# Cross-attention and feed-forward block: output weights loaded in pieces and split in the last batch, two output tiles projected inside the attention block

## The reference, cut to what matters

```python
q = layernorm(x) @ Wq;  k = ctx @ Wk;  v = ctx @ Wv      # per batch: 112x1024, 375x256, 375x256
out = softmax(q k^T / sqrt(32)) v                        # 4 query heads share one k, v head
x = x + out @ Wo                                         # Wo 1024x1024
x = x + w2( silu(w1 h) * (w3 h) ),  h = layernorm(x)     # width 3584, weights with block scales
```

## Time and profile before

| | us |
|---|---|
| median of three timed runs | 2510.64 |
| the three runs | 2515.27, 2510.57, 2510.64 |
| the profiled execution, whole | 2515.51 |
| its span | 2513.7 |
| PE busy in the span | 2423.2 (96%) |
| DVE, ACT, POOL busy | 1697.5, 979.4, 558.2 |

### The profile page before, as it was taken

How to read it: one execution, slowest core, us unless ns; L and a number is a source line. 1 busy time by engine, 2 the same in 40 slices (tenths; PEclk the granted TensorE clock), 3 DMA queues, 4 the chain that set the end, 5 groups by cost and what they waited for, 6 DMA issues and landing times.

```text
span 2513.7 us, 35414 instructions
## 1 busy us (share of the span) xinstructions
PE 2423.2 (96%) x12682; PEld 2068.6 (82%) x12682; DVE 1697.5 (68%) x2639; ACT 979.4 (39%) x1673; POOL 558.2 (22%) x305
## 2 busy tenths in 40 slices
PE   7998999999999799799999998999999989999999
PEld 7997878878876388699999987999888978888887
DVE  6425777777776445788888887888878874445442
ACT  3212445445454422444544445334443342323221
POOL 1000354454454400011111110332233320000000
PEclk9998999999998799899999999999999999999999
DMA  7534555455545345475565643766577687565652
GB/s 226 173 96 137 144 136 145 134 141 143 133 113 136 85 148 168 126 218 163 175 185 157 179 151 113 207 168 173 189 211 203 169 280 228 171 186 151 186 164 84
DMA packets 369147, 408.04 MB, mean 162 GB/s; under 512 B 125825, under 2 KB 324097, under 8 KB 359153
## 3 DMA queue, kind: packets, MB, share of 16 engines
q1 hardware_dynamic: 369008, 406.22, 56.6%
HBM read 252.99 MB, written 152.70 MB: 161 GB/s over the span
## 4 chain that ended last, share of the span: by engine, by line
PE 47%; DVE 4%; DMA 2%; issue 1%; SPq 0%; ACT 0%; DVEq 0%
PE bank L84 16%; PE bank L86 16%; PE bank L85 16%; DMA stash<-weight_scratch 2%; DVE g_WL L90 1%; DVE g_XL L90 1%; DVE g_su L1731 1%; DVE stash L1225 1%; DVE stash L1226 1%; DVE xT L1723 0%; SPq L1544 0%; DVE stash L1228 0%; ACT stash L1649 0%; DVE stash L1736 0%; ACT g_WH L1198 0%
## 5 line engine op out<-in xcount | busy, mean ns | idle before, releaser
L84 PE MATMUL bank<-g_XH,g_WH 128*128 128x448 f32 (+1 forms) x2254 | 847.1, 376 | 34.4 <-DVE g_su L1731 17.6
L85 PE MATMUL bank<-g_XL,g_WH 128*128 128x448 f32 (+1 forms) x2254 | 844.5, 375 | 0.0
L86 PE MATMUL bank<-g_XH,g_WL 128*128 128x448 f32 (+1 forms) x2254 | 844.4, 375 | 0.0
L84 PEld LDWEIGHTS bank<-g_XH,g_WH 128*128 128x128 f32 x2254 | 424.6, 188 | 98.4 <-DVE g_WL L90 22.4
L86 PEld LDWEIGHTS bank<-g_XH,g_WL 128*128 128x128 f32 x2254 | 424.6, 188 | 54.3
L85 PEld LDWEIGHTS bank<-g_XL,g_WH 128*128 128x128 f32 x2254 | 424.7, 188 | 54.0
L1198 ACT ACTIVATE g_WH<-stash 128x512 fp32r<-128x512 f32 x392 | 241.2, 627 | 420.9 <-PE bank L86 249.5
L90 DVE TENSOR_TENSOR g_WL<-stash,g_WH 128x512 fp32r<-128x512 f32 (+1 forms) x417 | 335.8, 809 | 77.2 <-ACT g_WH L1198 48.9
L696 DVE TENSOR_REDUCE a_nm<-bank 112x1 f32<-112x375 f32 x512 | 265.2, 532 | 116.8 <-PE bank L831 113.2
L800 ACT ACTIVATE a_pr<-bank 125x448 f32<-125x448 f32 x384 | 204.2, 545 | 205.8 <-PE bank L907 151.9
L649 POOL TENSOR_TENSOR a_prsum<-a_pr 125x1792 f32<-125x1792 f32 x32 | 129.4, 4043 | 362.2 <-ACT a_pr L800 362.2
(11 more groups left out here) (132 smaller groups left out, 3589.3 us busy)
## 6 DMA issues: line engine op xcount, KB each, us to landing
stash<-in_L_ffn_w SPq DMA_DIRECT2D x168, 256.0 KB, 5.2
weight_scratch<-stash SPq DMA_DIRECT2D x28, 1024.0 KB, 7.7
stash<-weight_scratch SPq DMA_DIRECT2D x28, 1024.0 KB, 7.4
h_scratch<-g_Sh SPq DMA_DIRECT2D x112, 224.0 KB, 4.0
down_scratch<-xT SPq DMA_DIRECT2D x98, 256.0 KB, 3.0
stash<-in_ctx SPq DMA_DIRECT2D x48, 500.0 KB
stash<-h_scratch SPq DMA_DIRECT2D x25, 896.0 KB, 6.4
a_qst<-q_scratch SPq DMA_DIRECT2D x96, 224.0 KB, 4.7
```

The costliest lines, as they stand in the source:

```text
L84: pe.matmul(acc, lh, rh, start=first, stop=False, skip_group_check=onto)
L85: pe.matmul(acc, lh, rl, start=False, stop=False, skip_group_check=onto)
L86: return pe.matmul(acc, ll, rh, start=False, stop=last, skip_group_check=onto)
```

## The change

The change has five parts.

1. The split copies of context, the key and value weights and the split keys, the split output weights (`wo_h`, `wo_l`), the split attention tiles and, later, the split activations of the feed-forward stage now lie in one tile, `work`, whose pieces follow one another in time. The split output weights take the place of the split context and the split key and value weights. As the keys no longer lie in one piece, they are stored with one DMA for each group: four per batch in place of two. One buffer of the feed-forward stage (`XL`, `BL_`) lies in two pieces.
2. The slots of the values move to rows 8 and 11 of `stash`.
3. `load_wo` is called three times: rows 0 to 2 in batch 12, rows 3 to 5 in batch 13, rows 6 and 7 in batch 14. SP loads attention tiles 0 and 1 and x tile 0 in batch 15.
4. DVE makes both parts of the output weights, in steps 15 to 22 of batch 15: a copy, then a subtraction, for each of the eight rows. Behind batch 15's steps it splits attention tiles 0 and 1 before it inverts the last sums, then tile 2. ACT makes the copies of those tiles.
5. PE projects tile 0 into banks 0 and 1 before the last sums and tile 1 into banks 4 and 5 after them, still in the attention block. The mixing block begins on PE with the products of tile 2, followed by the transposes of tiles 0 and 1.

The diff, cut to its core:

```diff
+                WO_AT = {15 + c: c for c in range(KT)}
...
+                            if isinstance(b, int) and b == B - 4:
+                                sp.wait_ge(t_done, NT * (B - 1))
+                                load_wo(sp, range(0, NC))
+                            if isinstance(b, int) and b == B - 3:
+                                sp.wait_ge(t_done, NT * B)
+                                load_wo(sp, range(NC, 2 * NC))
                             if isinstance(b, int) and b == B - 2:
-                                sp.wait_ge(t_done, NT * B)
                                 sp.wait_ge(v_moved, B)
-                                load_wo(sp)
+                                load_wo(sp, range(2 * NC, KT))
+                            if isinstance(b, int) and b == B - 1:
+                                sp.wait_ge(o_stored[0], 16 * (B - 2))
+                                sp.wait_ge(o_stored[1], 16 * (B - 2))
+                                sp.wait_ge(pv_done, NC * NG * (B - 1))
+                                load_attn(sp, 0)
+                                load_x(sp, 0)
+                                load_attn(sp, 1)
...
                                 for hl, buf in enumerate((k_h, k_l)):
-                                    sp.dma_start(k_scr[par, hl].rearrange("g p n -> p g n"),
-                                                 buf[:, :, :].bitcast(f32)).then_inc(k_stored, 16)
+                                    for g in range(NG):
+                                        sp.dma_start(k_scr[par, hl, g], buf[g].bitcast(f32)
+                                                     ).then_inc(k_stored, 16)
...
                         each(sp, body)
-                        sp.wait_ge(pv_done, NC * NG * (B - 1))
-                        load_tile(sp, 0)
                         store(B - 1, 0)
+                        sp.wait_ge(pv_done, NC * NG * B)
+                        load_x(sp, 1)
+                        sp.wait_ge(a_lo, 1)
+                        load_attn(sp, 2)
                         store(B - 1, 1)
...
+                        def split_wo(c):                                   # DVE
+                            if c == 0:
+                                dve.wait_ge(wo_loaded, 16 * R * KT)
+                                dve.wait_ge(v_done, NC * B)
+                            nc.vector.tensor_copy(wo_h[:, c, :], wo_raw[:, c, :]).then_inc(wo_hi, 1)
+                            dve.wait_ge(wo_hi, c + 1)
+                            to_lo(wo_l[:, c, :], wo_raw[:, c, :], wo_h[:, c, :]).then_inc(wo_lo, 1)
...
+                                if isinstance(b, int) and b == B - 1 and s in WO_AT:
+                                    split_wo(WO_AT[s])
                         each(dve, body)
+                        dve_split_attn(a_h, a_l, 0)
+                        dve_split_attn(a_h, a_l, 1)
                         for j in range(J):
                             invert(B - 1, 1, j)
+                        dve_split_attn(a_h, a_l, 2)
...
                         each(act, body)
+                        act.wait_ge(v_done, NC * B)
+                        act_split_attn(a_h, 0)
                         copy_out(B - 1, 1)
+                        act_split_attn(a_h, 1)
                         copy_sums(B - 1, 1)
+                        act_split_attn(a_h, 2)
...
+                        def project(t, acc):                               # PE
+                            pe.wait_ge(a_lo, t + 1)
+                            for c in range(KT):
+                                pe.wait_ge(wo_lo, c + 1)
+                                for n in range(2):
+                                    last = split_product(
+                                        pe, acc[n][:, :], (a_h[:, t, c, :], a_l[:, t, c, :]),
+                                        (wo_h[:, c, n * FB:(n + 1) * FB],
+                                         wo_l[:, c, n * FB:(n + 1) * FB]), c == 0, c == KT - 1)
+                                    if c == KT - 1:
+                                        last.then_inc(o_done, 1)
                         each(pe, body)
+                        project(0, s_bank)
                         sums(B - 1, 1)
+                        project(1, pj_bank)
...
                         for t in range(1, NT_TOK):                         # mixing, ACT
-                            if t + 1 < NT_TOK:
-                                split_attention(t + 1)
+                            if 1 < t < NT_TOK - 1:
+                                act_split_attn(a_h, t + 1)
                             out_x(t - 1)
...
                         residual_norm(0)                                   # mixing, DVE
                         for t in range(1, NT_TOK):
-                            if t + 1 < NT_TOK:
-                                split_attention(t + 1)
+                            if 1 < t < NT_TOK - 1:
+                                dve_split_attn(a_h, a_l, t + 1)
                             residual_norm(t)
...
-                                pe.wait_ge(y_done, 2 * t + n - 1)          # mixing, PE
+                                pe.wait_ge(y_done, n + 1 if t == 2 else 2 * t + n - 1)
...
-                        for t in range(1, NT_TOK):
+                        for t in range(2, NT_TOK):
                             products(t)
+                            if t == 2:
+                                transposes(0)
                             transposes(t - 1)
```

More of the change, by code:

```diff
@@ L144, in load_ctx, with load_wo @@
                              .rearrange("b k n -> k (b n)")).then_inc(c_loaded[slot], 16)
-        def load_wo(sp):
+        def load_wo(sp, cs):
             rows = wo.rearrange("(g r j d) n -> g j r d n", g=NG, r=R, j=J)
-            for c in range(KT):
+            for c in cs:
                 for r in range(R):
@@ L435, in _, with mix_views, act_split_attn, dve_split_attn @@
                                 last.then_inc(p_done, 1)
-        def attention():
+        def mix_views(work):
+            C = NG * J
+            w = [work[:, n * C * D:(n + 1) * C * D].rearrange("p (c n) -> p c n", n=D)
+                 for n in range(2)]
+            at = 2 * C * D
+            a = [work[:, at + n * 2 * C * P:at + (n + 1) * 2 * C * P].rearrange(
+                "p (s c q) -> p s c q", s=2, q=P) for n in range(2)]
+            return w + a
+        def act_split_attn(a_h, t):
+            nc.scalar.wait_ge(a_loaded[t % 2], 16 * (t // 2 + 1))
+            wait(nc.scalar, o_done, 2 * (t - 1))
+            nc.scalar.activation(a_h[:, t % 2, :, :], attn_in[:, t % 2, :, :], ACT.Copy
+                                 ).then_inc(a_hi, 1)
+        def dve_split_attn(a_h, a_l, t):
+            nc.vector.wait_ge(a_hi, t + 1)
+            to_lo(a_l[:, t % 2, :, :], attn_in[:, t % 2, :, :], a_h[:, t % 2, :, :]
+                  ).then_inc(a_lo, 1)
+        def attention(work):
             with ExitStack() as st:
@@ L941, in s_ @@
                     return sem(f"m_{name}")
[L942 to L943 removed]
+                w_h, w_l, a_h, a_l = mix_views(work)
                 yb, xn = sb("yb", [P, 2, D]), sb("xn", [P, 2, KT, P])
@@ L1105, in transposes, with ffn @@
                                 last.then_inc(t_done, 1)
-                        pe.wait_ge(a_lo, 1)
-                        for c in range(C):
-                            pe.wait_ge(w_lo, c + 1)
-                            for n in range(2):
-                                last = product(0, n, c)
-                                if c == C - 1:
-                                    last.then_inc(o_done, 1)
-                        for t in range(1, NT_TOK):
+                        for t in range(2, NT_TOK):
                             products(t)
+                            if t == 2:
+                                transposes(0)
                             transposes(t - 1)
                         transposes(NT_TOK - 1)
-        def ffn(xT):
+        def ffn(xT, work):
             with ExitStack() as st:
@@ L1824, in build_program @@
         queries()
-        attention()
-        with nc.sbuf_tensor("xT", [P, KT, HALF], f32) as xT:
-            ffn(xT)
+        with nc.sbuf_tensor("work", [P, 12 * KH * TB], f32r) as work:
+            attention(work)
+            with nc.sbuf_tensor("xT", [P, KT, HALF], f32) as xT:
+                ffn(xT, work)
 _INS = ['x', 'ctx_4096', 'L0_xattn_Wq', 'L0_xattn_Wk', 'L0_xattn_Wv', 'L0_xattn_Wo', 'L0_ffn_w1',
```

108 lines of the change are left out of this document (54 added, 54 removed).

## The result

The change makes the kernel slower. Timed beside the kernel before, the changed kernel took a median of 2528.07 us (2524.63 to 2530.95, four runs) against 2510.61 (2509.79 to 2515.27); the ratio is 1.0056, with a 95% interval of 1.0039 to 1.0073. A second comparison of the same two kernels, later and with more runs, gave 2522.80 us (seven runs) against 2512.65 (twelve): 1.0041, interval 1.0023 to 1.0058. The two ratios mean + 14 and + 10 us. The first ratio isn't the plain quotient of its two medians: that is 1.0070 (+ 17.5 us). Four runs a side are coarse here. The forecast was + 8.5 (2519.1 us, a ratio of 1.0034, range 2510 to 2525).

The account below looks back on a forecast made before the run. TensorE (PE), busy 96% of the span, was taken as the bound. Projection start + 3.8 us and start to tile 3 + 4.7 made + 8.5 on the 2510.64 us median: 2519.1 us, range 2510 to 2525.

Parts of the forecast that it names:

- DVE and POOL take turns, copies included: Last batch: DVE's weight copies and subtractions and POOL's additions exclude each other at SBUF, whole instruction by whole instruction.
- The sign given for it: Last batch in the changed profile: weight subtractions of 2 to 5 us for the first five, 1.2 for the last three.
- Start of the projection at 865.6: PE's first output projection product comes at 865.6 instead of 861.85, 3.8 us later, after PE has stood for 14.6 us.
- Tile 0, last sums, tile 1, boundary: PE after the projection's start: tile 0 12.6 us, last sums 0.96, tile 1 11.0, idle at the block's end 1.4.
- The kernel before, start to tile 3, 37.0 us: Projection on PE, first product to tile 3: 37.0 us before (898.83 - 861.85), 41.7 in the new structure, so + 4.7.
- The stall before tile 3, 4.75 us: Tile 2's end to tile 3's start: 4.75 us through ACT's copies and split, DVE's subtraction and residual addition; 2.7 is new.
- From tile 3 on the order is as before, and the delay goes to the end unchanged: From output tile 3 to the kernel's end: nothing further gained or lost, so the + 8.5 us stays.
- rival d: Projection's tile 0: PE's clock returns late after 14.6 us idle, + 9.4 on top, + 17.9, 2528.5 us; chance 0.06.
- Key stores, output weights in three pieces, at no cost: Batches: two more key stores each (0.46 us of SP each) and 32 weight loads, 24 of them earlier, cost nothing.
- (a): Last batch: DVE and POOL do not exclude one another, or in small pieces; PE starts at 849.3, - 7.8, 2502.8 us; chance 0.14.
- (b): Last batch: exclusion, but copies take no turn; start 862.4 to 864.3, + 5.3 to + 7.2, 2516 to 2518 us; chance 0.20.
- (c): Part of the exclusion, ScalarE's wait after tile 2 shorter (2.7 gone, boundary 0.7): + 2, 2512.5 us, no change; chance 0.10.

Follow-up runs that it names:

- The cut additions: Changed kernel with POOL's four additions of the last batch cut to one column in 448 (sums left out): 2509.95 us against 2513.69 for the kernel before.
- the second profile: The changed kernel unaltered, run and profiled again beside the kernel before: 2522.80 us (seven runs) against 2512.65, ratio 1.0041.
- the two experiments with 4.67: Changed kernel with attention tile 3 loaded earlier, or with seven feed-forward DMAs issued behind that load: 2519.33 and 2518.96 us; tile 2's end to tile 3's start 4.67 us.
- the four key stores: Kernel before with each batch's keys stored in four DMAs instead of two, nothing else changed: 2510.83 us beside a median of 2512.65.
- all of it: Changed kernel with ACT's weight copies, earlier split of tile 0, early load and split of tile 3, tile 2 in banks 6 and 7: 2506.15 us, ratio 0.9970.

## Why the prediction came out as it did

The direction and the first mechanism (the turns of DVE and POOL) were right, the size was too small: + 8.5 against + 10 to + 14 in the timed runs (+ 17.5 between the medians of the first comparison), + 13.3 in the traces. The first comparison's median of 2528.07 us lies above my range of 2510 to 2525, its ratio applied to 2510.64 (2524.7 us) and the second comparison's median (2522.80) within it. Step by step:

- **DVE and POOL take turns, copies included**: right. Forecast of the four additions 4.5 to 5.1 us, measured 4.78, 4.94, 4.17, 4.77, one of them below. The eight rows took 30.7 us, forecast 31.4 (829.97 to 861.4). Which instruction has to wait for an addition was nearly right in the walk: it had copies 1, 2 and 4 and subtraction 4 (counted from 0), and the trace has copies 1, 2 and 5 and subtraction 4. The sign given for it, subtractions of 2 to 5 us for the first five, did not follow from that walk and was wrong: only two were above 1.23. That a copy is as short as 0.69 us was right too, but not by the row alone: 551 ns for 768 columns, scaled by columns, gives 0.73. The cut additions are the proof of the mechanism: same instructions, 15 us less.
- **Start of the projection at 865.6**: 866.68 measured. Counted from batch 14, the start comes 3.6 and 2.3 us later than in the kernel before, against + 3.8. PE's wait there is 13.05 and 14.18 us, forecast 14.6.
- **Tile 0, last sums, tile 1, boundary**: 12.84 (13.31 in the second profile), 0.96, 11.0 and 1.33 us measured, against 12.6, 0.96, 11.0 and 1.4. Right.
- **The kernel before, start to tile 3, 37.0 us**: I took the end of the transposes (898.83) for the start of tile 3, which is 898.58. The way is 36.7 us, so my own terms give + 5.0 for + 4.7, and + 8.8 in all.
- **The stall before tile 3, 4.75 us**: this term failed. It was 8.00, and 7.66 in the second profile. The chain of ACT and DVE that it was built on is right to 0.1 us, as the two experiments with 4.67 show. Missing was the load of attention tile 3, for which I gave no arrival at all. In the kernel before it is issued at 888.35, 18.7 us after the first of the seven feed-forward DMAs (869.67); in the changed kernel, at 899.06, only 7.1 us after (891.95), since the whole new block opens at once behind tile 1. The loss is 3.25 and 2.9 us.
- **"From tile 3 on the order is as before, and the delay goes to the end unchanged"**: wrong by 2.9 and 1.8 us. The order is the same, but the clock isn't: the stall that I had counted, and more so the longer one, sent PE to its lower level. I had weighed the clock only for the 14.6 us ahead of tile 0 (rival d, which did not occur: tile 0 took 12.84), not for the stall that the change adds. Even at 4.67 us of stretch tile 3 took 12.6 instead of 11.0, so + 1.6 was to be had from my own forecast.
- **Key stores, output weights in three pieces, at no cost**: right over batches 8 to 13; batch 14 is open within 1 us.
- **Rivals**: (a) needed additions and DVE instructions side by side, and is excluded by the four waiting rows and by the run with short additions. (b) fell with the first waiting copy. (c) had the stall at 2.7 less, and the stall went the other way. (d) had 2528.5 us, next to the first median of 2528.07, but that is chance: its slow tile 0 of 22 us is not there, and the time was lost ahead of tile 0, ahead of tile 3 and in tile 3.

The two profiles sum up as follows, from batch 14 on: start of the projection + 3.6 and + 2.3 (forecast + 3.8), from there to tile 3 + 8.5 and + 8.7 (forecast + 4.7), tile 3 and what follows it + 2.9 and + 1.8 (forecast 0): + 15.0 and + 12.7.

## What to carry to other kernels

Before moving work into an engine's idle time, look at what the other engine of the shared path does at that moment: eight rows of 1.9 us placed among POOL additions of 4 us took 30.7 us, not 15, and the same subtractions with their copies on ACT took 21.4. For each place where a pipeline is cut and restarted, ask for the arrival of every operand, the loads too, and list what is ahead of them in the DMA queue; an order change on the waiting engine gains nothing while the load is late. And add to a new stall of PE the slower clock behind it.

## What the runs showed that I had not expected

**The feed-forward stage runs at one of two paces**, whatever the kernel. POOL's first addition of a pair of weights repeats every 34.72 us in the profile of before (1292.88, then 1327.60 of the earlier trace rows), and every 34.05 us in the second profile of the changed kernel:

```profile
1302.86 1.16 POOL L1673 TENSOR_TENSOR g_Sh<-stash 128x448 f32<-128x448 f32 x1 [27.99 <-DVE stash L1800]
1336.91 1.16 POOL L1673 TENSOR_TENSOR g_Sh<-stash 128x448 f32<-128x448 f32 x1 [27.99 <-DVE stash L1800]
```

From the last transposes to the end of DVE's long wait for a load near the middle of the stage (at 1553.68 before), that is 522.7 us before and 522.2 in the first profile of the changed kernel, but 514.8 in the second and 514.3 with the four key stores. PE is 100% busy from 1200 to 1400 us at a granted clock of 1.00 in either pace. All twelve profiles have one pace or the other, six each: 34.72 us where the table above has a rest of 1481.8 to 1482.8, and 34.05 where it has 1473.9 to 1476.5. Before, changed and all of it are among the slower six, so they can be compared as they are: spans of 2513.7, 2529.2 and 2504.4 us. Some 8 us of scatter come from this alone, nearly as much as the forecast difference; this may well be behind the spread of the kernel before (2507.24 to 2519.06) and the difference of the two comparisons, 1.0056 and 1.0041; I have the pace of the profiled runs only. What chooses the pace no run here shows. For a change of this size the traces up to the stage were the better measure than the time.

**A copy from float32 to the rounded format on DVE** takes 0.69 us for 1024 columns, as the prediction had it, and is kept waiting by POOL's additions as a subtraction is.
